# Moving two elementwise products and two rounding remainders from VectorE to GpSimd in a two-branch transformer layer

## The reference, cut to what matters

```python
# branch 1: gated linear recurrence, then an MLP
q, k, v, a, g = split(rms(xn) @ in_proj_w.T, 5)
q = rms_per_head(q); k = tanh(k); a = clip(sigmoid(a + 2), 0.6, 0.9995)
u = k * v
# in chunks of 64 tokens, the state carried from chunk to chunk:
#   prefix = cumprod(a); acc = cumsum(u / max(prefix, 1e-6)); states = prefix * (state + acc)
y = sigmoid(g) * (q * memory) + (1 - sigmoid(g)) * v
x1 = xn + 0.707 * (y @ out_proj_w.T)
x1 = x1 + 0.707 * (silu(rms(x1) @ fc_w.T) @ proj_w.T)
# branch 2: 8-bit activations and ternary weights
h = silu(depthwise_conv3(bit_linear(xn, w1)))
out = x + x1 + bit_linear(h, w2)
```

## Time and profile before

| what | value |
|---|---|
| median of the 2 runs shown | 8438.66 us (8328.6 and 8548.73) |
| the profiled execution's own time | 8401.61 us |
| its span on the slowest core (core 6) | 8400.1 us |
| spans of the 8 cores | 8262.3 to 8400.1 us |
| PE busy | 5159.6 us (61%) |
| DVE busy | 3115.2 us (37%) |
| ACT busy | 1169.4 us (14%) |
| POOL busy | 75.7 us (1%) |

### The profile page before, as it was taken

The page is one execution under the profiler, slowest core; times in us unless marked ns, Lnnn a source line. Parts: engine busy times, 40 slices in busy tenths (PEclk is TensorE's granted clock), DMA queues, the critical chain, the costliest instruction groups (busy, mean ns, idle before and its releaser), DMA issues.

```text
span 8400.1 us, 60803 instructions; the slowest of 8 cores (8262.3 to 8400.1 us)
## 1 busy us (share of the span) xinstructions
PE 5159.6 (61%) x20589; PEld 2148.8 (26%) x20995; DVE 3115.2 (37%) x5019; ACT 1169.4 (14%) x1521; POOL 75.7 (1%) x52
## 2 busy tenths in 40 slices
PE   3676536766367663278788588999989203442145
PEld 0232202322023220133233233444434101111012
DVE  3434444344444445444535411101010125553443
ACT  2111111111111112111111112011010002321000
POOL 0000000000000000000000000000000000000100
PEclk7788857887578886589888799999888656775577
DMA  1011110111101110200000102232222232221222
GB/s 49 24 47 63 45 43 26 45 57 52 43 23 48 53 51 0 68 18 18 18 16 18 55 18 83 93 98 92 90 77 85 98 107 93 76 82 62 86 70 88
DMA packets 173350, 478.23 MB, mean 57 GB/s; under 512 B 20148, under 2 KB 20472, under 8 KB 160760
## 3 DMA queue, kind: packets, MB, share of 16 engines
q1 hardware_dynamic: 173048, 474.31, 17.0%
HBM read 386.11 MB, written 88.09 MB: 56 GB/s over the span
## 4 chain that ended last, share of the span: by engine, by line
PE 52%; DVE 20%; DMA 13%; ACT 6%; issue 4%; DVEq 4%; SPq 1%; POOL 0%; ACTq 0%; POOLq 0%
PE ps L489 27%; PE ps L1071 9%; PE ps L1038 8%; DMA AR<-w1T 3%; DVEq L65 3%; PE ps L1360 3%; DMA AR<-w2T 3%; DMA AR<-sp_h 2%; DVE AR L446 2%; DVE AR L510 2%; ACT AR L442 2%; PE ps L330 2%; DMA AR<-wipT 1%; PE ps L326 1%; DVE AR L812 1%
## 5 line engine op out<-in xcount | busy, mean ns | idle before, releaser
L489 PE MATMUL ps<-AR 128*128 128x512 bf16 x10532 | 2455.0, 394 | 650.4 <-DVE AR L446 618.8
L489 PEld LDWEIGHTS ps<-AR 128*128 128x128 bf16 x10752 | 1081.5, 101 | 2035.3 <-issue 861.3
L446 DVE TENSOR_TENSOR AR<-AR 128x1024 bf16<-128x1024 f32 x184 | 225.3, 1224 | 1912.0 <-ACT AR L442 1912.0
L1038 PE MATMUL ps<-AR 128*128 128x512 bf16 x3010 | 698.6, 394 | 81.7 <-DVE AR L1020 78.0
L1071 PE MATMUL ps<-AR 128*128 128x512 bf16 x3011 | 721.7, 404 | 14.6 <-DVE AR L1050 10.5
L1194 PE MATMUL ps<-AR 128*128 128x512 bf16 (+1 forms) x1254 | 302.8, 400 | 395.8 <-DVE AR L1167 319.1
L1360 PE MATMUL ps<-AR 128*128 128x512 bf16 x1003 | 228.6, 389 | 493.1 <-DVE AR L1344 492.1
L1038 PEld LDWEIGHTS ps<-AR 128*128 128x128 bf16 x3072 | 309.3, 101 | 472.1 <-issue 189.2
L1071 PEld LDWEIGHTS ps<-AR 128*128 128x128 bf16 x3072 | 314.9, 103 | 421.4 <-issue 206.9
L510 DVE RECIPROCAL AR<-AR 128x2048 f32<-128x2048 f32 x32 | 414.5, 12953 | 3.3 <-issue 0.4
L330 PE MATMUL ps<-AR 128*1 128x512 f32 (+1 forms) x272 | 156.7, 662 | 295.9 <-ACT AR L322 295.9
(11 more groups left out here) (154 smaller groups left out, 3510.6 us busy)
## 6 DMA issues: line engine op xcount, KB each, us to landing
AR<-wipT SPq DMA_DIRECT2D x112, 512.0 KB, 3.5
AR<-sp_fchi SPq DMA_DIRECT2D x128, 256.0 KB, 2.6
AR<-sp_fclo SPq DMA_DIRECT2D x128, 256.0 KB, 2.9
AR<-sp_prhi SPq DMA_DIRECT2D x128, 256.0 KB, 2.6
AR<-sp_prlo SPq DMA_DIRECT2D x128, 256.0 KB, 2.9
AR<-w1T SPq DMA_DIRECT2D x64, 512.0 KB, 3.7
AR<-w2T SPq DMA_DIRECT2D x64, 512.0 KB, 3.5
sp_h<-AR SPq DMA_DIRECT2D x32, 1024.0 KB, 5.3
```

Of the source, the lines that this page charges most:

```text
L446: tl = vop(lambda E, h=hi, l=lo: E.tensor_tensor(out=l[:, 0:1024], in0=wsf[:, 0:1024], in1=h[:, 0:1024], op=OP.subtract), reads=("wsf",), ...
L489: E.matmul(o, l, r, start=a, stop=z),
L1038: E.matmul(o, l, r, start=a, stop=z),
```

## The change

Four operations go from DVE (`vop`) to POOL (`gop`): u in the prefix windows (24 times 128x2048 float32), u among the own tokens (8 times), `tyl` (8 times 128x2048, bfloat16 out) and `tf_last` (128 times 128x512, bfloat16 out). Since a program's order no longer keeps them apart from their neighbours on DVE, waits are added: u waits for the last reader of `r1(4)` in the pass before (`scan0`), the product L512 in `recurrence` waits for u (`uwait`), and five groups of DMAs wait for POOL's semaphore too. In the last stage the wait for the last block of w2 ahead of the first matmuls is replaced by a wait for each block ahead of the matmul that uses it, in the first output block only. The wait for the last block of the quantized h (`xq2_t[-1]`) stays where it was.

```diff
@@ recurrence
-                       reads=(tag + "u", tag + "p5"), writes=(tag + "u",))
+                       reads=(tag + "u", tag + "p5"), writes=(tag + "u",),
+                       wait=[uwait])
@@ prefix windows
-                    wait=[(sv, sv.n), (st, st.n), (ss, ss.n)])
+                    wait=[(sv, sv.n), (st, st.n), (ss, ss.n), (sg, sg.n)])
...
-                tu = vop(lambda E: E.tensor_tensor(out=r1(4, Twin), in0=r1(2, Twin),
+                tu = gop(lambda E: E.tensor_tensor(out=r1(4, Twin), in0=r1(2, Twin),
...
-                         wait=[ek[-1], ev[-1]])
+                         wait=[ek[-1], ev[-1], pxq.get("scan0")])
@@ own tokens
-            tu = vop(lambda E: E.tensor_tensor(out=r1(4, Town), in0=r1(2, Town),
+            tu = gop(lambda E: E.tensor_tensor(out=r1(4, Town), in0=r1(2, Town),
...
-                     wait=[ek[-1], ev[-1]])
+                     wait=[ek[-1], ev[-1], prv.get("scan0")])
...
-            tyl = vop(lambda E, o=ylo(c, Town), h=yhi(c, Town): E.tensor_tensor(
+            tyl = gop(lambda E, o=ylo(c, Town), h=yhi(c, Town): E.tensor_tensor(
                 out=o, in0=r1(0, Town), in1=h, op=OP.subtract),
-                reads=(tag + "q", f"yl{c}"), writes=(f"yl{c}",), wait=[tyh])
+                reads=(tag + "q", f"yl{c}"), writes=(f"yl{c}",), wait=[tyh, y4])
@@ MLP
-                tf_last = vop(lambda E, o=tflo(hc, gw), i=bc1(gw), h=tfhi(hc, gw):
+                tf_last = gop(lambda E, o=tflo(hc, gw), i=bc1(gw), h=tfhi(hc, gw):
@@ last stage
-                fw = bank(b, extra=[xq2_t[-1]]
-                          + ([w2q_t[-1]] if gi == 0 else []))
+                fw = bank(b, extra=[xq2_t[-1]])
                 tmm = None
                 for kc in range(NHID):
                     a = (kc == 0)
                     z = (kc == NHID - 1)
+                    ww = (fw if a else [])
+                    if gi == 0 and oc == 0:
+                        ww = ww + [w2q_t[kc]]
...
-                              wait=(fw if a else ()))
+                              wait=ww)
```

More of the change, by code:

```diff
@@ L495, in mm3, with recurrence @@
             return etoks
-        def recurrence(T, nck, with_carry, tag, cidx, carry_only=False):
+        def recurrence(T, nck, with_carry, tag, cidx, carry_only=False, uwait=None):
             t1 = r1(1, T)
@@ L527, in recurrence @@
                       reads=(tag + "a",), writes=("gq",))
-            vop(lambda E: E.tensor_copy(out=hq, in_=av[:, :, CH - 1]),
-                reads=(tag + "u",), writes=("hq",))
+            thq = vop(lambda E: E.tensor_copy(out=hq, in_=av[:, :, CH - 1]),
+                      reads=(tag + "u",), writes=("hq",))
             vop(lambda E: E.tensor_tensor(out=hq, in0=hq, in1=gq, op=OP.mult),
@@ L563, in recurrence @@
                 tmem = tgq
+            u4last = tmem if not carry_only else thq
             vop(lambda E: E.tensor_tensor_scan(
@@ L566, in recurrence @@
                 reads=("gq",), writes=("gq",))
-            return gq[:, nck - 1:nck], Ssc[:, nck - 1:nck], tdiv, tmem
+            return gq[:, nck - 1:nck], Ssc[:, nck - 1:nck], tdiv, tmem, u4last
         fc_jobs = [("fc", d_wfc[hc], d_fchi[hc], d_fclo[hc]) for hc in range(NHID)]
@@ L646, in build_program @@
                     wait=[ea[-1]])
-                A_ap, B_ap, rdiv, rmem = recurrence(Twin, nWCH, False, tag, c,
-                                                    carry_only=True)
-                pxq = {"u": tu, "mem": rmem}
+                A_ap, B_ap, rdiv, rmem, ru4 = recurrence(Twin, nWCH, False, tag, c,
+                                                         carry_only=True, uwait=tu)
+                pxq = {"u": tu, "mem": rmem, "scan0": ru4}
                 Am = s_cry[:, 4 * nWCH + 2:4 * nWCH + 3]
@@ L861, in build_program @@
                 wait=[ea[-1]])
-            _, _, rdiv, rmem = recurrence(Town, nCHK, True, tag, c)
+            _, _, rdiv, rmem, ru4 = recurrence(Town, nCHK, True, tag, c, uwait=tu)
             eg = mm3(Town, ghi, glo,
@@ L872, in build_program @@
                 pend[f"k{c + 1}"] = prep2(d_wip[8 + c + 1], "k")
-            vop(lambda E: E.tensor_tensor(out=r1(0, Town), in0=r1(0, Town),
-                                          in1=r1(4, Town), op=OP.mult),
-                reads=(tag + "q", tag + "u"), writes=(tag + "q",))
+            y1 = vop(lambda E: E.tensor_tensor(out=r1(0, Town), in0=r1(0, Town),
+                                               in1=r1(4, Town), op=OP.mult),
+                     reads=(tag + "q", tag + "u"), writes=(tag + "q",))
             vop(lambda E: E.tensor_tensor(out=r1(0, Town), in0=r1(0, Town),
@@ L900, in build_program @@
                 writes=(f"yh{c}",), wait=[y4] + ([SPLT] if c == 0 else []))
-            tyl = vop(lambda E, o=ylo(c, Town), h=yhi(c, Town): E.tensor_tensor(
+            tyl = gop(lambda E, o=ylo(c, Town), h=yhi(c, Town): E.tensor_tensor(
                 out=o, in0=r1(0, Town), in1=h, op=OP.subtract),
-                reads=(tag + "q", f"yl{c}"), writes=(f"yl{c}",), wait=[tyh])
-            prv = {"u": tu, "mem": rmem, "y3": y3, "y4": y4, "yd": tyl}
+                reads=(tag + "q", f"yl{c}"), writes=(f"yl{c}",), wait=[tyh, y4])
+            prv = {"u": tu, "mem": rmem, "y3": y3, "y4": y4, "yd": tyl,
+                   "scan0": y1}
         EMIT3 = stop_after >= 3
@@ L911, in build_program @@
                 dma(r1(c, Town), d_sxn[c * 128:(c + 1) * 128, 1:1 + Town],
-                    wait=[(sv, sv.n), (st, st.n), (ss, ss.n), (spl, spl.n)]))
+                    wait=[(sv, sv.n), (st, st.n), (ss, ss.n), (spl, spl.n),
+                          (sg, sg.n)]))
         pos = {0: prep2(d_wop[0], "op"), 1: prep2(d_wop[1], "op")}
@@ L1139, in build_program @@
             td = dma(bc1(TH), d_xown[c * 128:(c + 1) * 128, :],
-                     wait=[(sv, sv.n)], sem=s_rx)
+                     wait=[(sv, sv.n), (sg, sg.n)], sem=s_rx)
             vop(lambda E, o=r1(c, Town), i=bc1(TH)[:, 1:1 + Town]:
```

## The result

The changed kernel is slower: the ratio is 1.0169, with a 95% interval of 1.0111 to 1.0227. The compared executions lie at 8469 to 8488 us after and, but for one, at 8312 to 8329 us before; many others of either kernel had one die at a lower clock, so that the medians over all (8808 and 8477 us) say nothing of the change. The profiled execution after took 8490.07 us, with 8488.5 on its slowest core, against 8401.61 before.

The account below looks back on a forecast made before the run. It took chains between engines, none full, as the bound. Terms 79 + 5 + 17 + 3 = 104 us gave 8506 from the profiled 8401.6 or 8543 from the median; forecast 8525 us (+1.2%), range 8410 to 8640.

Parts of the forecast that it names:

- What bounds the kernel: Whole kernel: no engine is full, time lies in chains between engines; u on DVE costs nothing today.
- How long POOL takes: POOL's 128x2048 operation: 4.4 us, from reckonings of 3.8, 5.1 and 4.2; ends 3.8 and 5.1.
- Blocking: Prefix windows: POOL's u makes DVE's L446 stand still, PE starts a 3.3 us later, 24 times: 79 us.
- no blocking: Rival, prefix windows: L446 runs beside POOL, u is free, only `tyl` and `tf_last` cost: 8422 us; chance 0.12.
- POOL is much slower: Rival, 2048-column operations: POOL needs 6.3 us or more; at 7 us, 8590 or 8627 us; chance 0.09.
- DVE was the bound: Rival, whole kernel: all 180 us moved off DVE leave the path, giving 8222 us; chance 0.03.
- The clock: a's matmuls in prefix passes: PE's longer gap changes their starting clock level; 5 us, ends -9 and +16.
- 18 gain 0.5: Clock term: 18 of 24 prefix passes, at about 23.7 us, gain 0.5 us each if 6.6 idle acts as 7.41.
- u among the own tokens: Own tokens: u meets an L446 readying g one product ahead, so 0; without that cover 26 us.
- tyl: Own tokens, before q's readout: on the path, 4.4 us on POOL for 2.29, 8 times: 17 us.
- tf_last and the finer waits: Projection: last `tf_last` of each group delays it, 3 us; last stage: finer waits release nothing, 0.
- The base: Starting time for the sum: midway between the profiled 8401.6 us and a two-run median 37 us above.

Follow-up runs that it names:

- delayed u: Kernel before with only u of the 24 prefix passes on POOL, made to wait for L446; profiled execution 8332.75 us, no ratio.
- halved u: Kernel before with 1024 of 2048 columns of the prefix passes' u on POOL, the rest on DVE behind L446; ratio 1.0068.
- `tyl` alone: Kernel before with only `tyl` on POOL, plus the change's waits on tokens; 8467 us, own tokens 1254 us on cores 2 and 3.

## Why the prediction was right, and where it was off

- *What bounds the kernel.* The reading that u costs nothing on DVE, since DVE idles 20.9 us behind it, held: 73 us of u left DVE, and nothing got faster.
- *How long POOL takes.* 4.4 us was taken, 4.50 and, with a bfloat16 result, 4.05 were measured. Of the three reckonings twice 1024 columns (4.2) lay closest to 4.50. POOL began 0.20 us after ACT's readout, not 0.14.
- *Blocking.* This was the step left unseen in the trace of before. L446 ended 1.07 us after POOL where 1.08 was forecast, and PE's gap grew by 3.44 where 3.3 was: 83 us for 79. The delayed u and the halved u show it as a cause. So the rival *no blocking* fell. *POOL is much slower* fell too, as did *DVE was the bound*.
- *The clock.* This term was mis-sized: 5 us forecast, about 20 measured. The step that failed is "18 gain 0.5". The slower 18 runs of core 6 took 23.5 us on average before and not 23.7 (three took 22.57, which the earlier trace rows do not show), and a run behind the gap of 6.78 took 23.4, not 23.2. So the 18 gained 0.1 each and the six lost 2.5, which makes 14 us on that core. On other cores more runs had full clock to lose (11 of 24 on core 2 and 18 on core 7 of the kernel before).
- *u among the own tokens.* 0, as forecast, with L446 held and unnoticed.
- *tyl.* 17 forecast, about 16 measured. Some 5 us beside it have no known cause: with `tyl` on DVE the own tokens took 1237 to 1239 us on all cores where the prefix u waits for L446, and 1233 is usual. The added waits do not explain it, as the expectation for `tyl` alone took it: the run with half of u has the same waits there and took 1232 to 1234. The granted clock over the stretch was 0.863 to 0.866 in the one and 0.866 to 0.874 in the other; what set it is open.
- *tf_last and the finer waits.* 3 forecast, 4 measured; PE's gap ahead of the projection went from 2.62 to 3.12 us, four times. The finer waits did nothing (351 to 355 us before, 353 to 357 after).
- *The base.* The sum of 104 us was set on a base of 8420; with what was measured it is 83 + 20 + 16 + 5 + 4 = 128. The executions compared lie at about 8320: the profiled one carried 59 us of slow MLP on its slowest core, and the higher of the two runs shown was no measure. So the base was 100 us too high and the sum 50 too low against the 155 measured, and the forecast of 8525 came out only 50 us above the 8473 by two errors of opposite sign. That it came so close was luck; that the kernel got slower, and by which mechanism, was not.
- *What no term had.* Of about 155 us, some 25 lie in none of these terms. 22 of them lie between the last a and the first q, where each core loads its own x (469 to 480 us before and 488 to 508 after, on the table's cores). POOL is not needed for them: 492 to 499 show too with the weights of a readied early, where nothing is on POOL but what was. The twelve profiled executions show what goes with them. Cores 0 and 1, 2 and 3, 4 and 5, 6 and 7 make 48 pairs; where the two of a pair ended their windows 29 us or more apart, the stretch took 469 to 476 us, at 16 to 23 us apart 474 to 486, and within 3 us 492 to 514. In the kernel before, cores 0 and 1 ended 0.1 us apart and took 514. In the 50 us behind its window core 0 got 92 GB/s there, and core 2, whose neighbour ended 30 us later, 123. The changed kernel makes the windows of all cores alike (2838 to 2851 us, where before they took 2698 to 2807), and its pairs ended 1 to 9 us apart. That the loads of a pair fall together and share what they get fits all this; it was not tried by an experiment. The 7 us in the out projection may be of the same kind (293 to 294 us on cores 0 and 1 of the kernel before, 287 to 289 on the others). They and the 5 us beside `tyl` stay open.

## What to carry to other kernels

Before an elementwise operation goes to GpSimd, look not at how busy VectorE is but at what VectorE will do at that very moment, and who waits for it. A product that lay idle behind a critical operation can, on another engine, start ahead of it. Where the move is wanted all the same, a wait can put it behind the critical operation; here one such wait undid the loss of the prefix passes. Taking the critical operation out of the chain was worth more than the move could ever have been.

## What the runs showed of the hardware

- A DVE tensor_tensor with two SBUF inputs stands still while a GpSimd tensor_tensor runs, and ends 1.07 to 1.08 us after it for its own 1.23. Seen at POOL durations of 2.35, 4.50 and 4.51 us. This is the rule of the Trainium skill (SBUF — State Buffer, section SBUF: two separate sides), and the numbers agree with it.
- A float32 reciprocal on DVE, with one input, took 12.95 us beside a GpSimd product as it does alone, and the product 4.51. The same rule of the Trainium skill names only two-input and two-port operations as held, and this agrees too.
- GpSimd's product of 128x2048 in float32 took 4497 ns in the median, to the nanosecond what the Trainium skill gives for an add of that size (GPSIMD Engine Reference, section Elementwise, side-by-side cycle accounting). With a bfloat16 result it took 4054; 1024 columns in float32 took 2345.
- Behind a gap of 4.68 us no run of a's matmuls kept full clock, in 24 passes on each of eight cores, nor did any behind 6.78 us; behind 3.34 us, in the kernel before, it was 3 to 18 of 24, differing from core to core.
- The stretch in which both cores of a pair load their x was 469 to 476 us long where they began 29 us or more apart and up to 514 where they began together.
